# A mixture-of-experts layer in split float32: the second product's correction in the columns of its own sum

## What is computed

```
s0 = relu(x @ swi[0]) @ swo[0]                  # swi: 256 x 1024, swo: 1024 x 256
s1 = relu(x @ swi[1]) @ swo[1]
eo = relu(x @ wi[itok]) @ wo[itok]              # one of 5 experts, chosen by sample
w  = softmax(relu(concat(eo[:,0], s0[:,0], s1[:,0]) @ g1) @ g2)     # three gates per sample
y  = x + eo*w[0] + s0*w[1] + s1*w[2]
out = y + zX*laplace_x(y) + zY*laplace_y(y) + zR*y*(1 - y)
```

## Time and profile before

| | |
|---|---|
| median of 3 runs | 1193.63 us (1193.39 to 1194.26) |
| the profiled execution | 1192.88 us |
| its span, first to last instruction | 1191.0 us |
| mean granted TensorE clock | 0.995 of full speed |
| PE matmuls / weight loads | 6124 / 6124 |
| DVE busy, ACT busy, POOL busy | 56%, 39%, 6% of the span |

### The profile page before, as it was taken

The page is one execution under the profiler, slowest core; times in us unless marked ns, Lnnn a source line. Parts: engine busy times, 40 slices in busy tenths (PEclk is TensorE's granted clock), DMA queues, the critical chain, the costliest instruction groups (busy, mean ns, idle before and its releaser), DMA issues.

```text
span 1191.0 us, 16700 instructions
## 1 busy us (share of the span) xinstructions
PE 1164.8 (98%) x6124; PEld 992.0 (83%) x6124; DVE 672.7 (56%) x1008; ACT 460.2 (39%) x802; POOL 72.5 (6%) x105
## 2 busy tenths in 40 slices
PE   5999999999999999999999999999999999999995
PEld 4888888888889998888888888888888888888884
DVE  6655555555557763555555565465465465465455
ACT  3445444444545652332423333333333233333232
POOL 3101110110112200000000000000000000000001
PEclk9999999999999999999999999999999999999998
DMA  7644453444446633022022022021021021021110
GB/s 230 182 124 129 145 152 111 145 148 129 118 140 187 218 109 93 10 54 62 5 58 63 1 62 54 9 63 45 18 62 45 18 63 45 18 63 36 27 27 27
DMA packets 39041, 98.09 MB, mean 82 GB/s; under 512 B 8368, under 2 KB 15536, under 8 KB 38960
## 3 DMA queue, kind: packets, MB, share of 16 engines
q1 hardware_dynamic: 26720, 52.98, 16.3%
q0 software_dynamic: 12096, 44.05, 12.5%
q10 hardware_dynamic: 144, 0.00, 0.0%
HBM read 75.24 MB, written 17.56 MB: 78 GB/s over the span
## 4 chain that ended last, share of the span: by engine, by line
PE 95%; DVE 2%; DMA 1%; SPq 1%; issue 0%; ACT 0%; DVEq 0%; ACTq 0%
PE acc L717 31%; PE acc L718 15%; PE hbank L693 15%; PE hbank L692 15%; PE hbank L694 15%; PE tbank L656 2%; DMA g1s<-in_L_cond_g 1%; PE tbank L657 1%; DMA xs<-in_x 0%; SPq L915 0%; SPq L903 0%; PE acc L706 0%; PE tbank L664 0%; DVE rows L350 0%; DMA itk<-in_itok_B 0%
## 5 line engine op out<-in xcount | busy, mean ns | idle before, releaser
L471 DVE SCALAR_TENSOR_TENSOR hl<-hbank,hh 128x512 fp32r<-128x512 f32 (+1 forms) x424 | 278.0, 656 | 437.9 <-ACT hh L781 437.7
L781 ACT ACTIVATE hh<-hbank 128x512 fp32r<-128x512 f32 (+1 forms) x424 | 241.6, 570 | 621.0 <-PE hbank L694 617.3
L717 PE MATMUL acc<-swo,hh 128*128 128x512 f32 x1024 | 370.9, 396 | 0.0
L718 PE MATMUL acc<-swo,hl 128*128 128x256 f32 x1024 | 286.9, 280 | 0.0
L717 PEld LDWEIGHTS acc<-swo,hh 128*128 128x128 f32 x1024 | 192.3, 188 | 45.5 <-DVE eo L489 0.2
L717 PE MATMUL acc<-ewo,hh 128*128 128x512 f32 x560 | 205.1, 397 | 0.2
L692 PE MATMUL hbank<-xh,swh 128*128 128x512 f32 x512 | 204.8, 400 | 0.0
L693 PE MATMUL hbank<-xl,swh 128*128 128x512 f32 x512 | 202.2, 395 | 0.0
L718 PEld LDWEIGHTS acc<-swo,hl 128*128 128x128 f32 x1024 | 193.1, 189 | 10.0
L694 PE MATMUL hbank<-xh,swl 128*128 128x512 f32 x512 | 199.7, 390 | 0.0
L718 PE MATMUL acc<-ewo,hl 128*128 128x256 f32 x560 | 157.3, 281 | 0.0
(11 more groups left out here) (164 smaller groups left out, 873.7 us busy)
## 6 DMA issues: line engine op xcount, KB each, us to landing
rw<-in_L_cond_wi POOLq DMA_DIRECT2D x42, 512.0 KB, 4.4
rw<-in_L_cond_wo POOLq DMA_DIRECT2D x42, 512.0 KB, 5.3
xs<-in_x SPq DMA_DIRECT2D x140, 64.0 KB, 2.9
eo_scratch<-eo SPq DMA_DIRECT2D x140, 64.0 KB, 2.7
xs<-in_x SPq DMA_DIRECT2D x16, 512.0 KB, 5.2
ei<-eo_scratch SPq DMA_DIRECT2D x16, 512.0 KB, 6.6
out<-ot SPq DMA_DIRECT2D x15, 512.0 KB, 3.8
y<-y SPq DMA_DIRECT2D x32, 120.0 KB
```

The lines of the kernel that those rows point to most:

```text
L471: e.scalar_tensor_tensor(HL[:, g % NH, 0:w], bank[:, 0:w], 0.0, HH[:, g % NH, 0:w].bitcast(F32), ALU.max, ALU.subtract).then_inc(h_lo, 1)
L717: e.matmul(acc[j][:, 0:2 * D], HH[:, g % NH, js], woc[:, c, :], start=(c == 0), stop=False)
L718: m = e.matmul(acc[j][:, D:2 * D], HL[:, g % NH, js], woc[:, c, 0:D], start=False, stop=last)
L781: e.activation(HH[:, g % NH, 0:w], hbank[g % HRING][:, 0:w], ACT.Relu).then_inc(h_hi, 1)
```

## The change

The 512-column matmul of a block becomes two of 256 columns, and all three matmuls of a block add into the same 256 columns. A bank then holds two blocks side by side: blocks 0 and 1 in one bank, 2 and 3 in the next, and passes take turns between banks 0, 1 and banks 2, 3 (acc_place). Only the first matmul in a bank has start set. The last pass keeps one block a bank, with columns 256 to 511 unused. ACT alone copies a bank of two blocks to EO with one operation, and DVE's additions of the correction are gone (L485, L489). The two PRE passes get banks 0 and 2, and semaphores of their own for their copies to S01.

```diff
+def acc_place(n, j):
+    return (j, 0) if n == NP - 1 else (2 * (n % 2) + j // 2, j % 2 * D)
...
@@ DVE @@
-                for j in block_order(n):
-                    e.wait_ge(acc_hi, ACC[n, j] - 2)
-                    if kind == EXP:
-                        dst = EO[i % 2][:, j, :]
-                        e.tensor_tensor(dst, acc[j][:, D:2 * D], dst, ALU.add).then_inc(acc_free, 1)
-                    else:
...
-                        e.scalar_tensor_tensor(dst, acc[j][:, D:2 * D], WB[:, 1 + b, t:t + 1], dst,
-                                               ALU.mult, ALU.add).then_inc(acc_free, 1)
...
+            def add_last(j):
+
+                y = inner(NT - 1)[:, j, :]
+                e.wait_ge(acc_free, ACC[NP - 1, j])
+                e.wait_ge(dve_seq, V.n)
+                e.tensor_tensor(y, y, EO[1][:, j, :], ALU.add).then_inc(*V.up())
...
+                if (n, c) in ((1, LAG - 1), (2, LAG - 1)):
+                    e.wait_ge(s01_prod, n)
+                    e.tensor_copy(S01[:, n - 1, :], acc[2 * (n - 1)][:, 0:D]).then_inc(s01_done, 1)
+                if g == G + LAG - 1:
+                    for j in LAST_ORDER:
+                        add_last(j)
@@ PE, second_product @@
-                    if c == 0 and acc_before(n, j):
-                        e.wait_ge(acc_free, acc_before(n, j))
-                    e.matmul(acc[j][:, 0:2 * D], HH[:, g % NH, js], woc[:, c, :], start=(c == 0), stop=False)
-                    m = e.matmul(acc[j][:, D:2 * D], HL[:, g % NH, js], woc[:, c, 0:D], start=False, stop=last)
-                    if last:
+                    bank, at = acc_place(n, j)
+                    to = acc[bank][:, at:at + D]
+                    if c == 0 and at == 0 and acc_before(n, bank):
+                        e.wait_ge(acc_free, acc_before(n, bank))
+
+                    e.matmul(to, HH[:, g % NH, js], woc[:, c, 0:D], start=(c == 0 and at == 0), stop=False,
+                             skip_group_check=True)
+                    e.matmul(to, HH[:, g % NH, js], woc[:, c, D:2 * D], start=False, stop=False,
+                             skip_group_check=True)
+                    m = e.matmul(to, HL[:, g % NH, js], woc[:, c, 0:D], start=False, stop=last,
+                                 skip_group_check=True)
+                    if last and (n == NP - 1 or at == D):
                         m.then_inc(acc_done, 1)
@@ ACT, evacuate, expert units @@
-                        e.activation(EO[i % 2][:, j, :], acc[j][:, 0:D], ACT.Copy).then_inc(acc_hi, 1)
+                    for m in range(blocks(n) // 2):
+                        bank = acc_place(n, 2 * m)[0]
+                        e.wait_ge(acc_done, ACC[n, bank])
+                        e.activation(dst[:, 2 * m:2 * m + 2, :].rearrange("p j d -> p (j d)"), acc[bank][:],
+                                     ACT.Copy).then_inc(acc_free, 1)
@@ ACT, evacuate, shared passes @@
-                    e.wait_ge(acc_done, ACC[n, j])
-                    e.activation(EO[b][:, j, :], acc[j][:, 0:D], ACT.Copy,
-                                 scale=WB[:, 1 + b, t:t + 1]).then_inc(acc_hi, 1)
+                for m in range(2):
+                    bank = acc_place(n, 2 * m)[0]
+                    e.wait_ge(acc_done, ACC[n, bank])
+                    e.activation(dst[:, 2 * m:2 * m + 2, :].rearrange("p j d -> p (j d)"), acc[bank][:], ACT.Copy,
+                                 scale=scale).then_inc(acc_free, 1)
```

More of the change, by code:

```diff
@@ L51, in block_order, with acc_before, acc_last @@
     return LAST_ORDER if n == NP - 1 else range(blocks(n))
+def acc_place(n, j):
+    return (j, 0) if n == NP - 1 else (2 * (n % 2) + j // 2, j % 2 * D)
 ACC = {}
-for _n in range(NP):
+for _n in range(2, NP):
     for _j in block_order(_n):
-        ACC[_n, _j] = len(ACC) + 1
-def acc_before(n, j):
-    return max([ACC[m, j] for m in range(n) if (m, j) in ACC], default=0)
+        if (_n, acc_place(_n, _j)[0]) not in ACC:
+            ACC[_n, acc_place(_n, _j)[0]] = len(ACC) + 1
+def acc_before(n, bank):
+    return max([ACC[m, bank] for m in range(n) if (m, bank) in ACC], default=0)
+def acc_last(n):
+    return max(v for (m, _), v in ACC.items() if m == n)
 def tile_parts(n, c):
@@ L701, in second_product @@
                 if PASSES[n][0] == PRE:
-                    if c == 0 and n > 0:
-                        e.wait_ge(acc_free, acc_before(n, 0))
                     if c % 4 == 0:
                         e.wait_ge(w_in[n][2 + c // 4], 16)
-                    e.matmul(acc[0][:, 0:D], HF[:, g % NH, :], raw(n, 2 + c // 4)[:, c % 4, :],
-                             start=(c == 0), stop=last).then_inc(acc_done if last else h_used, 1)
+                    e.matmul(acc[2 * n][:, 0:D], HF[:, g % NH, :], raw(n, 2 + c // 4)[:, c % 4, :],
+                             start=(c == 0), stop=last).then_inc(s01_prod if last else h_used, 1)
                     return
@@ L784, in evacuate @@
                 kind, i = PASSES[n]
[L785 to L790, removed]
[L791 to L802 removed]
+                t, b = i // 2, i % 2
@@ new lines, in evacuate @@
+                dst, scale = EO[b], WB[:, 1 + b, t:t + 1]
+                if t == 0:
+                    e.wait_ge(eo_out[b], ST_VAL[NU - 1 if (NU - 1) % 2 == b else NU - 2])
+                    e.wait_ge(t_free, T_AT["spread"])
+                else:
+                    e.wait_ge(dve_seq, AT["shared", t - 1, b])
+                if n == NP - 1:
+                    for j in LAST_ORDER:
+                        e.wait_ge(acc_done, ACC[n, j])
+                        e.activation(dst[:, j, :], acc[j][:, 0:D], ACT.Copy, scale=scale).then_inc(acc_free, 1)
+                    return
@@ L921, in store_unit @@
                 n = 2 + u
[L922 removed]
+                e.wait_ge(acc_free, acc_last(n))
                 for b in range(k):
```

40 lines of the change are left out of this document (17 added, 23 removed).

## The result

The changed kernel takes 1196.32 us (median of 18 runs, 1194.75 to 1197.43), the kernel before 1193.69 us on the same chips (18 runs, 1192.18 to 1194.87). The ratio is 1.0021, with a 95% interval of 1.0014 to 1.0027: 2.6 us slower. The forecast had the sign and the side of the stream right, and more than twice the loss.

What follows compares the result with a forecast made beforehand. The prediction took TensorE's own instruction stream as the bound: +7.4 us stream, -0.3 gate, -1.2 tail make +5.9, giving 1199.5 us (0.5% slower); forecast band 1195.5 to 1204.7, overall range 1191.5 to 1207.

Steps and rivals of the forecast that it cites:

- What bounds the kernel: Between 40 and 1177 us TensorE's own instruction stream sets the time; removing semaphores there is worth nothing.
- The cost of an added matmul: Second product: 5 ns per added matmul, on 1472 blocks of 512-wide chunks only, +7.4 us, bounds 0 and 11.1.
- The Trainium skill's fixed 2.5 ns: Cross-check on the second product's stream: 1584 added matmuls at 2.5 ns would cost 4.0 us in place of 7.4.
- PE's wait for a bank: At pass changes, alternating bank pairs move the wait for a freed bank back a pass; nothing gained, no such wait listed.
- The gate: Before the gate, DVE's two adds leave the chain and PE's wait goes: -0.3 us, bounds 0 and -0.4.
- Off the path: ACT's wider copies (598 ns) and DVE's lost operations are not waited for by PE: costed at nothing.
- The tail: At the program's end four L489 go, POOL ends earlier and the add on QQ follows: -1.2 us, bounds -0.5 and -1.9.
- A (half is half): Second product: a 256 costs exactly half a 512, so the stream stays; 1192.1 us, no change; chance 0.14.
- D: Weight loads are TensorE's bound: 1584 more make 1290 us of loads, time 1293 us; chance 0.02.
- B: Second product faster: the 512-wide full-bank matmul causes the extra cost, mean step below 0.116, 1184.7 us; chance 0.08.
- C: Second product: loads show in runs of twelve 256s, 0.12 a step, chunk 2.82, 1206.8 us; chance 0.10.

Runs made afterwards that it cites:

- x2: The changed kernel with each shared-pass block again one 512-column and one 256-column matmul, the copying out of banks as changed; shared sums not the reference's: 1188.18 us.
- x11: The changed kernel with 64 unused bytes between SWO and HH, and the first product's 512-column matmuls also cut in two of 256: 1188.48 us.
- x1: The changed kernel with 64 unused bytes before SWO and 64 behind it, so that SWO alone moves within a 128-byte block: 1186.32 us.
- x5: The changed kernel with 64 unused bytes before SWH and 64 after SWO, so that SWH and SWL move with SWO: 1180.61 us.
- x10: The kernel before the change, with 64 unused bytes between SWO and HH: 1194.09 us.

## Why the prediction was wrong

**What bounds the kernel: right in the main.** Nearly all that changed lies in the pitch of PE's stream; "no semaphore that the change removes there is worth anything" missed 1.6 us, of which more below. x2 gives back 8.1 us by PE's instructions alone.

**The cost of an added matmul: this is the step that failed.** I took "5 ns, the value of the nearest row, on the 512-wide chunks only" and got +7.4 us. Per block it is +0.034 / 4 = +8.5 ns in shared passes and -0.026 / 4 = -6.5 ns in large units: 8.7 - 2.9 - 1.0 = +4.8 us where I had 7.4. The total hides that there is no such price. The run of six 256s that I measured at 0.118 stands between 512s, in a small unit, at distance 64; a run of twelve settles, behind its first steps, at 0.113 there and at 0.120 at distance 0. In all, the twelve take 1.386 us in large units, where the eight before took 1.409, and 1.432 us in shared passes, where the eight took 1.400. My bounds, 0 and 11.1 us for both kinds together, did not leave room for a gain in one stage and a loss in the other. That the total of 1196.32 us still lies in my band is owed to these cancelling. The band itself, 1195.5 to 1204.7, does not come out of the bounds of my terms either: together they give 1191.3 to 1204.2. The rows already held a hint: L718's step is 0.11 in one place of the earlier trace rows and 0.12 in the other, and I made a rival of it where it called for a look at every position of a chunk, in both stages.

**The Trainium skill's fixed 2.5 ns** per matmul, in "TensorE: Matmul & The Clock Gate", section "Back-to-back issue gap", is given there for a matmul by itself and not for a stream of loads and matmuls. It would have given +2.5 us in all, close to the 2.6 measured, and by luck: one column count has steps of 113.3, 118 and 120.0 ns here.

**PE's wait for a bank: wrong in its reading.** "Nothing is gained, since no such wait shows in rows 3" missed 1.6 us, which lay under the modelled end of a matmul. The steps between starts, the measure that I used for everything else, show it.

**The gate: right**, 0.3 us. **Off the path: right**; ACT's wide copies take 599 ns in expert units and 689 with the gate as scale in shared passes (598 was the estimate), and TensorE waits for none of them.

**The tail: half.** I had -1.2 and bounds of -0.5 and -1.9; it is -0.5, the lower bound. POOL did what I said: it ends 1186.09 - 1180.97 = 5.12 us after the first ACT copy, where I had 5.1. What failed here is that the add on QQ would start at POOL's end. DVE is not ready for it: its four adds go on alternating with POOL at 0.97 us (3.33 us for the four) and end at 1184.81, and L547 and L549, 1.13 and 0.68 us, still stand before the add on QQ, which starts 0.67 us after POOL's end. So only the first L489 came off the chain. The rows of the kernel before had it already: there the add started at 1183.42, 0.64 us after POOL's end (1182.13 + 0.65).

**Rivals.** A (half is half) fell, since shared chunks rose by 0.034 us and those of large units fell by 0.026. D fell: loads are busy 1068.5 us, not 1290, and the kernel lost 2.6 us and not 99. B and C gave a mean step below 0.116 and one of 0.12. Their figures are both met, each in its stage: C's in shared passes (2.820, its own figure), B's in large units (1.386 / 12 = 0.1155). I had set them as alternatives for the whole kernel. Their reasons, the full-bank matmul and the load that shows, are not shown by that: the distance moves the same form from the one figure to the other.

**What stays open.** Why the distance counts is not shown. PE is busy 98% of the span and its loads 89%, so a load is read from SBUF while another array is streamed, and that is where I would look; whether it is the load or the stream that waits, what the first product's arrays have to do with the second's pace, and why a run settles at one, no run here tells. The Trainium skill, "SBUF — State Buffer", section "Who interferes with whom", gives TensorE one read port for the moving operand and an independent one for the weight load, and lets TensorE wait for nobody. With independent ports the places should be worth nothing; they are worth 16 us (1196.32 and 1180.19), so the measurement decides.

## What to carry to other kernels

Where TensorE's stream is the bound, measure starts against starts, in each stage by itself, and treat the place of the loaded operand against the streamed one in SBUF as a tunable like any other: here one unused array of 64 bytes a partition between SWO and HH made a change that lost 0.2% into one that gains 1.1% on the kernel before (x7, 1180.19 us). A wait shorter than the profile's modelled tail of a matmul does not appear among the waits; look for it in the steps at pass boundaries. A cut that pays in one product (x7) can cost in its neighbour (x11, +8.3 us), so try each alone.

## What the hardware showed that I had not expected

- A 256-column fp32r matmul with its load settles in the second product at 113.3 ns a step where loaded and streamed array begin 64 bytes apart within 128 bytes, and at 120.0 where they begin at the same place, with a granted clock of 1.00 in both stretches. Shared chunks take 2.760 us at 64, 2.820 at 0 and 2.807 at 32.
- The pace of the second product depends on the arrays of the first: with SWO, HH and HL alike, shared chunks take 2.787 (x1) or 2.760 us (x5).
- The mixed form of 512 and 256 columns takes 2.786 us a chunk at distance 0 and at distance 64, though its two products change by 9 ns each, one up and one down.
- 256-column matmuls can beat 512-column ones for the same columns: at distance 64 twelve of them take 1.386 us (x7), and the four 512s and four 256s that they replace 1.409 (x10).
